# Macaron block on one core: results of a token half taken out of the banks before the slot's attention and in two parts, attention spread over twelve slots, square sums on ScalarE

## What is computed

```python
x = x + 0.5 * ffn(layernorm(x))     # W1, W3: 512 -> 2048, silu(gate) * lin, Walsh-Hadamard, W2: 2048 -> 512
x = x + attn(layernorm(x))
x = x + 0.5 * ffn(layernorm(x))

def attn(x):                        # 8 batches x 512 tokens x 512, 16 heads of 32, chunks of 128 tokens
    h = rmsnorm(x, qkv_norm_w)
    q, k, v = h @ ternary(qkv_w).T
    # per chunk, with state S:
    o = scale * ((q k^T * mask) v + (q * lam_t) S);  S = lam_T * S + (k * lam_rev)^T v
    out = rmsnorm(o, norm_w, 1e-6)              # mean of squares of o
    return rmsnorm(out, proj_norm_w) @ ternary(proj_w).T
```

## Time and profile before

| | us |
|---|---|
| median of 3 runs | 2448.92 |
| lowest, highest | 2445.56, 2452.41 |
| the profiled execution's own time | 2448.42 |
| its span in the trace | 2446.7 |
| TensorE busy | 2324.2 (95%) |
| VectorE busy | 1615.1 (66%) |
| ScalarE busy | 858.2 (35%) |

### The profile page before, as it was taken

How to read it: one execution, slowest core, us unless ns; L and a number is a source line. 1 busy time by engine, 2 the same in 40 slices (tenths; PEclk the granted TensorE clock), 3 DMA queues, 4 the chain that set the end, 5 groups by cost and what they waited for, 6 DMA issues and landing times. The chain is left out here.

```text
span 2446.7 us, 48749 instructions
## 1 busy us (share of the span) xinstructions
PE 2324.2 (95%) x19551; PEld 1777.5 (73%) x19551; DVE 1615.1 (66%) x3644; ACT 858.2 (35%) x1749; POOL 214.2 (9%) x206
## 2 busy tenths in 40 slices
PE   9999999899999999898999998999989998999998
PEld 5444444578777877777887887888767877878887
DVE  7678466666776567756776577766776576657544
ACT  7644233233333333233333333333233323333222
POOL 0380033100000000000000000000000000000000
PEclk9999999999999999999999999999999999999999
DMA  9866432452544434534353335543553435243322
GB/s 243 218 168 178 123 104 70 151 123 70 135 120 131 98 84 127 137 94 112 98 157 96 93 119 142 123 103 90 153 115 100 112 103 140 78 114 87 107 87 63
DMA packets 351714, 291.57 MB, mean 119 GB/s; under 512 B 253824, under 2 KB 278656, under 8 KB 348672
## 3 DMA queue, kind: packets, MB, share of 16 engines
q1 hardware_dynamic: 351056, 287.66, 44.5%
q10 hardware_dynamic: 432, 0.79, 0.1%
HBM read 173.02 MB, written 59.77 MB: 95 GB/s over the span
## 5 line engine op out<-in xcount | busy, mean ns | idle before, releaser
L1893 PE MATMUL d_bank<-w2t,work 128*128 128x256 f16 x2496 | 383.7, 277 | 41.2 <-DVE work L1501 13.9
L1471 DVE SCALAR_TENSOR_TENSOR work<-l_bank,l_scale,work 128x256 f32<-128x256 f32 x416 | 181.7, 478 | 231.6 <-PE l_bank L1861 225.6
L1861 PE MATMUL g_bank<-work,w1t 128*128 128x256 f16 x2688 | 316.3, 275 | 12.8 <-ACT work L1131 12.8
L1861 PE MATMUL l_bank<-work,w3t 128*128 128x256 f16 x2688 | 311.7, 273 | 0.0
L1893 PEld LDWEIGHTS d_bank<-w2t,work 128*128 128x128 f16 x2496 | 241.0, 99 | 89.2 <-issue 42.2
L1861 PEld LDWEIGHTS g_bank<-work,w1t 128*128 128x128 f16 x2688 | 263.7, 99 | 52.2 <-ACT work L1131 14.5
L1861 PEld LDWEIGHTS l_bank<-work,w3t 128*128 128x128 f16 x2688 | 261.8, 98 | 31.5
L1893 PE MATMUL d_bank<-work 128*128 128x256 f16 x1872 | 277.8, 276 | 0.0
L1861 PE MATMUL g_bank<-xt,w1t 128*128 128x256 f16 x2304 | 271.0, 275 | 6.1 <-ACT work L1131 6.0
L1488 DVE TENSOR_TENSOR work<-work 128x256 f16<-128x256 f32 (+1 forms) x416 | 257.1, 618 | 20.9 <-ACT work L1143 20.9
L1861 PE MATMUL l_bank<-xt,w3t 128*128 128x256 f16 x2304 | 267.2, 273 | 0.0
(11 more groups left out here) (292 smaller groups left out, 2901.4 us busy)
## 6 DMA issues: line engine op xcount, KB each, us to landing
work<-w_dram SPq DMA_DIRECT2D x208, 384.0 KB, 3.3
work<-parts_dram SPq DMA_DIRECT2D x192, 128.0 KB, 2.9
x_dram<-work SPq DMA_DIRECT2D x16, 1024.0 KB, 4.8
parts_dram<-q_parts SPq DMA_DIRECT2D x32, 256.0 KB, 2.1
parts_dram<-k_parts SPq DMA_DIRECT2D x32, 256.0 KB, 2.4
norm_dram<-cent SPq DMA_DIRECT2D x32, 256.0 KB, 2.2
w2t<-in_L_ffn_W_dram SPq DMA_DIRECT2D x31, 256.0 KB, 3.3
xin<-in_L_attn_x_dram SPq DMA_DIRECT2D x7, 1024.0 KB, 8.5
```

The costliest lines, as they stand in the source:

```text
L1471: nc.vector.scalar_tensor_tensor(out=tokens, in0=l_bank[:, HALF * e:HALF * (e + 1)], scalar=l_scale[:, tile:tile + 1], in1=tokens, op0=ALU ...
L1861: ins = nc.tensor.matmul(dst[:, HALF * e:HALF * (e + 1)], wt[:, wp, k, P * tile:P * (tile + 1)], f.x[:, s_half, xp, k, :], start=(k == 0 a ...
L1893: ins = nc.tensor.matmul(bank_m[:, cols], combos[:, q % 2, hp, combo, :], weights[:, wp, :], start=(p == 0 and opens and hp == wp), stop=( ...
```

## The change

1. **hout in two parts.** `hout` keeps the ScalarE copy, L1498, L1501, L1507 and GpSimd's two additions; the last three VectorE steps are a new step `hend`. `hout` now stands directly behind the last `hdown` of the half, ahead of the D slot's attention; `hend` stands where all of it stood, behind that slot.
2. **back** is issued behind `hlin` of p = 7 of its own half, where before it came behind slot L of the next half, or at the end of the pass.
3. **Twelve slots.** Relative to `at`: scores at 0, 2, 4, 6 (before 0, 1, 3, 4), pv at 3, 5, 7, 9 (before 3, 4, 5, 6), q at -7 (before -6), k stays at -5, the loads of q (`qspread`, before a part of `klow` at -4) at -3, in front of those of k. `ostat`, the output norm and so on begin 3 slots later, `proj` is 1 slot later, the norm of the second feed-forward where it was. The norm of the first feed-forward of batch 6 goes from slot 364 to 353.
4. **Square sums.** The 64 bn_stats of `ostat` (8 per batch, L1568 and L1571) go from VectorE, and five of the small operations of `stat` with them; ScalarE runs 64 squares with an accumulated sum instead, each of which VectorE's scaling L1569 waits for, or which wait for it.
5. Pass 2 loses a special case, and the residual of passes under 3 takes its buffers from `tokens_out`.

The core of the diff:

```diff
@@ feed_forward
-                if n == 2 and j == 1:
-                    steps += in_slot + rest[0] + [("sclow", (0, 0, 1))] + rest[1]
-                else:
-                    steps += rest[0] + rest[1] + in_slot
+                steps += rest[0] + rest[1] + in_slot
@@ fast_feed_forward
+                    if which == "ffn2" and not last and p == PAIRS - 1:
+                        steps += [("back", (batch, s_half))]
...
-                    if which == "ffn2" and not last and s_half and p == 0:
-                        steps += [("back", (batch, 0))]
...
                     elif s_half:
-                        steps += [("hdown", (0, PAIRS - 1))] + slots.get(slot + 2, []) + [("hout", 0), ("resid", 0), ("resid", 1)]
+                        steps += [("hdown", (0, PAIRS - 1)), ("hout", 0)] + slots.get(slot + 2, [])
+                        steps += [("hend", 0), ("resid", 0), ("resid", 1)]
                     elif n > FAST:
-                        steps += [("begin", n - 1), ("hdown", (1, PAIRS - 1)), ("begin", n)] + slots.get(slot + 2, [])
-                        steps += [("begin", n - 1), ("hout", 1), ("resid", 2), ("resid", 3), ("begin", n)]
+                        steps += [("begin", n - 1), ("hdown", (1, PAIRS - 1)), ("hout", 1), ("begin", n)] + slots.get(slot + 2, [])
+                        steps += [("begin", n - 1), ("hend", 1), ("resid", 2), ("resid", 3), ("begin", n)]
@@ attention_slots
-                    add(slots, at - 6, [("q", (b, g))])
-                    add(slots, at - 5, [("qlow", (b, g)), ("k", (b, g))])
...
+                    add(slots, at - 7, [("q", (b, g))])
+                    add(slots, at - 6, [("qlow", (b, g))])
+                    add(slots, at - 5, [("k", (b, g))])
...
+                    add(slots, at - 3, [("qspread", (b, g)), ("kspread", (b, g))])
...
-            for at, b in ((19, 3), (109, 4), (253, 5), (364, 6), (461, 7)):
+            for at, b in ((19, 3), (109, 4), (253, 5), (353, 6), (461, 7)):
@@ scalar
+            def square_sum(a, t, scaled):
+                i = squares_before(t, scaled)
+                if scaled:
+                    act.wait_ge(o_scaled, TT * a + t + 1)
+                if i >= 2:
+                    act.wait_ge(o_stats, 2 * TT * a + i - 1)
+                sums = o_squares[:, TT * scaled + t:TT * scaled + t + 1]
+                nc.scalar.activation(squares_out[:, i % 2], x2[:, t, :], ACT.Square, accum_out=sums).then_inc(o_stats, 1)
@@ vector, ostat
-                    nc.vector.bn_stats(stat[:, t, :], x2[:, t, :]).then_inc(o_stats, 1)
+                    dve.wait_ge(o_stats, 2 * TT * a + squares_before(t, 0) + 1)
                     nc.vector.tensor_tensor(x2[:, t, :], x2[:, t, :], nw_row[:], ALU.mult).then_inc(o_scaled, 1)
-                    dve.wait_ge(o_scaled, TT * a + (t + 1))
-                    nc.vector.bn_stats(stat[:, TT + t, :], x2[:, t, :]).then_inc(o_stats, 1)
```

More of the change, by code:

```diff
@@ L321, in feed_forward @@
                 steps += [("w2sums", PAIRS - 1)]
-            return steps
+            return steps + ([("back", (batch, 0)), ("back", (batch, 1))] if which == "ffn2" else [])
         def fast_feed_forward(n, slots):
@@ L344, in fast_feed_forward @@
                     elif s_half:
-                        steps += [("hdown", (0, PAIRS - 1))] + slots.get(slot + 2, []) + [("hout", 0), ("resid", 0), ("resid", 1)]
+                        steps += [("hdown", (0, PAIRS - 1)), ("hout", 0)] + slots.get(slot + 2, [])
+                        steps += [("hend", 0), ("resid", 0), ("resid", 1)]
                     elif n > FAST:
-                        steps += [("begin", n - 1), ("hdown", (1, PAIRS - 1)), ("begin", n)] + slots.get(slot + 2, [])
-                        steps += [("begin", n - 1), ("hout", 1), ("resid", 2), ("resid", 3), ("begin", n)]
+                        steps += [("begin", n - 1), ("hdown", (1, PAIRS - 1)), ("hout", 1), ("begin", n)] + slots.get(slot + 2, [])
+                        steps += [("begin", n - 1), ("hend", 1), ("resid", 2), ("resid", 3), ("begin", n)]
                     else:
                         steps += slots.get(slot + 2, [])
-            if which == "ffn2" and not last:
-                steps += [("back", (batch, 1))]
             if last:
-                steps += [("hdown", (1, PAIRS - 1)), ("hout", 1), ("resid", 2), ("resid", 3)]
+                steps += [("hdown", (1, PAIRS - 1)), ("hout", 1), ("hend", 1), ("resid", 2), ("resid", 3)]
             return steps
@@ L380, in attention_slots @@
                 for g in range(GROUPS):
-                    add(slots, at - 6, [("q", (b, g))])
-                    add(slots, at - 5, [("qlow", (b, g)), ("k", (b, g))])
+                    add(slots, at, [("kv", (b, g)), ("score", (b, g, 0)), ("sclow", (b, g, 0)), ("state", (b, g))])
+                    add(slots, at + 1, [("statestore", (b, g)), ("statespread", (b, g))])
+                    add(slots, at + 2, [("score", (b, g, 1)), ("sclow", (b, g, 1))])
+                    add(slots, at + 3, [("pv", (b, g, 0))])
@@ new lines, in attention_slots @@
+                    add(slots, at + 4, [("score", (b, g, 2)), ("sclow", (b, g, 2))])
+                    add(slots, at + 5, [("pv", (b, g, 1))])
+                    add(slots, at + 6, [("score", (b, g, 3)), ("sclow", (b, g, 3))])
+                    add(slots, at + 7, [("pv", (b, g, 2))])
+                    add(slots, at + 9, [("pv", (b, g, 3))])
+                    at += GROUP_PERIOD
+                at -= GROUP_PERIOD * GROUPS
+                for g in range(GROUPS):
+                    add(slots, at - 7, [("q", (b, g))])
+                    add(slots, at - 6, [("qlow", (b, g))])
+                    add(slots, at - 5, [("k", (b, g))])
@@ L390, in attention_slots @@
[L390 to L395, removed]
@@ L396, in attention_slots @@
-                    end = at + 2 + TT
+                    end = at + 9
                     at += GROUP_PERIOD
@@ L401, in attention_slots @@
                 for t in range(TT):
-                    add(slots, end + 11 + t, [("proj", (b, t))])
+                    add(slots, end + 9 + t, [("proj", (b, t))])
                 add(slots, end + 1, [("projload", b)])
-                add(slots, end + 11 + TT, [("keep", b)])
+                add(slots, end + 9 + TT, [("keep", b)])
                 for t in range(TT):
-                    add(slots, end + 12 + t, [("rows", (("ffn2", b), t))])
-                norm(end + 12 + TT, ("ffn2", b))
+                    add(slots, end + 10 + t, [("rows", (("ffn2", b), t))])
+                norm(end + 9 + TT, ("ffn2", b))
             add(slots, 4, [("early", 3)])
@@ L558, in filled, with squares_before @@
             return USES[step, arg]
+        def squares_before(t, scaled):
+            return max(2 * t - 1, 0) if not scaled else 2 * t + (2 if t < TT - 1 else 1)
         def copied(step, arg, b):
@@ L823, in _ @@
                                            k_parts[:].rearrange("p a t -> p (a t)")).then_inc(k_turned, 16)
+                elif step == "qspread":
+                    ag = arg[0] * GROUPS + arg[1]
                     if ag:
```

55 lines of the change are left out of this document (32 added, 23 removed).

## The result

The changed kernel runs in 2384.89 us (median of 4 runs, 2381.87 to 2389.25), the kernel before in 2449.09 (2445.56 to 2452.41). The ratio is 0.9739 with a 95% interval of 0.9718 to 0.9761: 64 us faster. The forecast was 38 us faster, 2411 us, in a range that ended at 2390.

A forecast was written before the change was run, and what follows sets the result against it. TensorE is busy 2324.2 of 2446.7 us, so all the gain must lie in its 122.5 us of standstill. Terms: 65.3 us gained, 27 lost, 38 net, so 2448.9 - 38 = 2411 us; range 2390 to 2440.

The forecast's parts named there:

- (a): hout ahead of the slot at 13 half boundaries: of 34.5 us of waits 6.8 stay, 27.7 us gained.
- (b): Attention over twelve slots: two slots always lie between two pv that share a bank; 12.5 us gained.
- (c): The keys: with hout in front, ScalarE's copy for hout no longer waits for k; 9 us gained.
- (d): Start of pass 3: output norm comes later, a transposition moves away from 1 MB loads; 6.3 us gained.
- (e): Square sums moved to ScalarE: VectorE ends sooner behind ostat and stays within the pair; 6.4 us gained.
- (f): k waited for the copy of q; hlin now lies between them; 3.4 us gained.
- (g): q of group 0, now in front of hlin, waits longer for the qkv norm's transpositions; 22 us lost.
- (h): SP queue: the spreads of q have less room, 2 us lost; back issued earlier, 3 us lost.
- (1): Rival: VectorE is late anyway, so removed waits turn into the next ones; 2437 us, chance 0.20.
- Rival (2): The norm chain comes sooner and q of group 0 loses only 9 us; 2398 us, chance 0.09.
- (3): Rival: GpSimd's additions beside VectorE's slot work stretch steps with two SBUF inputs; 2425 us, chance 0.09.
- Case (5): hout stands ahead but VectorE reaches it no sooner; 2439 us, or 2448 without the keys' gain; chance 0.06.

The follow-up runs named there:

- e11: The kernel before with only hout in two parts and in front of the slot, nothing else changed: 2434.0 us, ratio 0.9939.
- e1: The changed kernel with hout whole behind the D slot again: 2404.5 us, ratio 0.9824.
- e3: The changed kernel with the attention, norm and projection slots of the kernel before: 2411.1 us, ratio 0.9857.
- e2: The changed kernel with the square sums on VectorE again (bn_stats): 2398.3 us, ratio 0.9803.
- e5: The changed kernel with q of group 0 behind hlin again, its norm where it is: 2368.0 us, ratio 0.9682.
- e4: The changed kernel with the qkv norms of batches 1 to 6 one slot earlier: 2383.7 us, ratio 0.9748.
- e8: On top of e5, hend ahead of the norm's prep at the six boundaries whose D slot holds one: 2371.9 us, ratio 0.9688.
- e7: The changed kernel with three useless bn_stats on VectorE in front of hout in each of eight halves: 2399.0 us, ratio 0.9808.

## Why the prediction was wrong, step by step

| step | waits before | forecast after | measured after |
|---|---|---|---|
| (a) hout | 34.5 | 6.8 | 15.5 |
| (b) pv | 12.8 | 0.3 | 4.4 |
| (c) keys | 13.1 | 4 | 8.0 |
| (d) start of pass 3 | 10.3 | 4 | 0.6 |
| (e) silu behind ostat | 8.4 | 2 | 2.3 |
| (f) k behind q | 3.4 | 0 | 0 |
| (g) q of group 0 | 9.1 | 31 | 22.7 |
| (h) spreads, back | 3.6 | 8.6 | 0.7 |
| sum | 95.2 | 57 | 54.2 |

The measured (a) is the rows of L1554 (9.5 and 3.7 us) and L1535 (2.0 and 0.3). The sum of the waits came out 3 us from the forecast, and the rows outside of it moved by 1 us. Idle time fell by 41 us where 38 were forecast. That this is so near is luck: (a), (b), (c) and (e) together left 17 us more waiting than forecast, (d), (g) and (h) 20 us less.

**The step that failed** is the sentence that all the change can give is in the 122.5 us in which TensorE stands still. It took busy time for work, and put the clock at nothing: the text ahead of the prediction has it at its upper level throughout, while 26.8 us were lost at the lower one. A wait that goes takes 0.17 us of busy time with it, some of the waits take a stretch of the lower clock with them, and the old order of pv and score held short stalls that are counted as busy. That was 24.3 us, and with the measured 41 us it gives 65.4, the difference of the two profiled executions. The range fell short for the same reason: its low end was made from waits alone.

**(a)** was over-sized by 9 us. The plain boundaries were right: eight boundaries wait 0.54 to 0.89 us each, where 0.8 was kept for six. The "2 us for the other seven together" was wrong: three boundaries inside a norm or ahead of one wait 3.4, 3.8 and 3.4 us, since the norm's prep stands between hout and hend and is slowed beside GpSimd (1.56 us twice, 1.01 us once, 0.75 alone). And e11 shows that 0.6 of the 1.5 us that a plain boundary gained are due to the slots, which the step did not say.

**(b)** left out that VectorE, with hend and a score behind it to do, is late for the second pv after a boundary: six waits of 0.73 us, in e1 too. **(c)** was right on the mechanism: e11 alone takes 7.6 us of the keys' waits away. Three waits of 2.0 to 3.1 us stay, one of which is in a pass ahead of the halves and is the same in both kernels, 2.9 and 3.1. **(d)** was under-sized: both waits went, not one and a bit. e3 shows that it is the slots that do it.

**(e)** came out right in its own row, 2.3 against 2, but undoing the squares costs 13.5 us and not 6.4. VectorE's 45 us fewer help at many places, each by 1 to 4 us, as e2's rows show. I had looked for the effect only where the operations stand.

**(f)** was right for its row, but left out the bank's other user: q of the next group now waits for a score's mask, 4.7 us in 5 places (L1710).

**(g)** is right in kind and over-sized: 13.6 us lost, not 22. e5 puts a price on it: 17 us come back when q stands behind hlin, 12 of them waits. **(h)** had the wrong sign. The spreads waited 3.6 us before and 0.7 now; the six transfers fit in the pair that was left to them, and the early back cost nothing that a row shows. It was never undone by itself, so what it is worth is not shown. The one wait for a w2 load grew from 1.2 to 3.2 us; no back is in flight there.

**The rivals.** VectorE late anyway (1) didn't come true as a whole, yet e4 and e8 show it at work where a step was put into slots that are already full. Rival (2) lies half-way: q lost 13.6 us, between its 9 and the forecast's 22. GpSimd's contention (3) is real at boundaries inside a norm, 0.8 us for L1641 at 746.29 us, but there are few. The slower case (4) was off by all of its price. Case (5) is out: hout's waits fell by 19 us. What the signs said held in part: q's row was to be near 30 us and is 22.7, VectorE near 1570 and is 1570.3, ScalarE near 910 and is 905.7, the parts_dram row under 8 and is 0.7; the row for hout was to be under 10 and is 15.5.

## What to carry to other kernels

Busy time of TensorE is not work time. Before summing waits, look at how long the same group of matmuls takes with and without a wait behind it, at what the weight loads wait for, and at the granted clock in fine windows. A mean of 0.987 was 27 us here. Here 40 us of listed waiting less brought 17 us of clock and pipeline ends with them in the profiled executions; in e5 it was 4 us for 12, in e1 10 us for 10.

When a product waits for a chain of other engines, put other matmuls in front of it (e5, 17 us) before moving the chain forward: moving the chain loads slots that are full, and the wait comes up elsewhere (e4, nothing; e8, which puts another step ahead of the chain, the same).

Cost an engine that is late at many places by what its work does everywhere: taking 45 us off VectorE was worth 13.5 us, twice what the place of the removed operations showed.

## What the runs showed of the hardware

A VectorE operation with two inputs from SBUF took 1.56 us instead of 0.75 beside a GpSimd addition, and that addition took 1.64 instead of 1.27. A VectorE operation that reads a bank took 0.48 us beside the same addition, as alone. After waits of TensorE, the longest of them 1.1 to 6.2 us, the granted clock was at 1.2 GHz for some 3.4 or 6.8 us (once 10), which cost 1.5 to 2.3 us of TensorE's time in the mean of a kernel. The same waits were followed by it at one place and not at another: five boundaries of the kernel before have 0.65, 1.38 and 1.60 us, and the clock fell after one of them (1337 us) and stayed at 2.4 GHz after four (1956 us among them). In e7 five boundaries have 0.79 and 1.38 us; it fell after four and stayed after the one near 1296 us, where two more waits of 0.73 and 1.07 us came behind. These runs don't tell what decides it.
